# Token lists of six experts in a mixture-of-experts stage: the marks as moving operand through four column strips

## What is computed

```python
capacity = max(1, int(Sz * CAP_FACTOR / E) + 1)          # 313 of 1250
scores = jax.nn.softmax(jnp.einsum('bsd,ed->bse', x, router_w), axis=-1)
gate_vals, sel_idx = jax.lax.top_k(jnp.swapaxes(scores, 1, 2), capacity)
tokens = x[b_idx, sel_idx]
h = jax.nn.gelu(jnp.einsum('becd,edh->bech', tokens, w1) + b1[None, :, None, :], approximate=False)
y = jnp.einsum('bech,ehd->becd', h, w2) + b2[None, :, None, :]
out = jnp.zeros_like(x).at[b_idx, sel_idx].add(y * gate_vals[..., None])
```

## Time and profile before

| | us |
|---|---|
| median of 3 runs (lowest, highest) | 1502.46 (1500.67, 1502.67) |
| the profiled execution | 1499.6 |
| its span, first to last instruction | 1497.5 |
| TensorE busy | 1422.4 (95%) |
| VectorE busy | 883.5 (59%) |
| ScalarE, GpSimd busy | 544.7, 357.6 |
| mean granted TensorE clock | 0.986 of 2.4 GHz |
| expert stage, from the first layer of expert 0 to the end | 1255.4 to 1497.5 |
| one expert of the first six | 29.19 |

### The profile page before, as it was taken

How to read it: one execution, slowest core, us unless ns; L and a number is a source line. 1 busy time by engine, 2 the same in 40 slices (tenths; PEclk the granted TensorE clock), 3 DMA queues, 4 the chain that set the end, 5 groups by cost and what they waited for, 6 DMA issues and landing times.

```text
span 1497.5 us, 28303 instructions
## 1 busy us (share of the span) xinstructions
PE 1422.4 (95%) x8379; PEld 726.7 (49%) x8379; DVE 883.5 (59%) x1992; ACT 544.7 (36%) x756; POOL 357.6 (24%) x372
## 2 busy tenths in 40 slices
PE   6789999999999999999999999999999979999996
PEld 5334444545444444444654444446544435666653
DVE  7888888686987887541442222223336676576652
ACT  4578757373524543210111210001111124565651
POOL 4332320202201110000874002800012311343232
PEclk9999999999999999999999999999999999999998
DMA  7242010000275555553323443430046756789963
GB/s 282 43 86 51 8 43 14 28 0 28 72 205 155 159 168 174 144 142 112 128 72 90 103 101 125 170 114 12 0 128 177 203 190 200 218 250 273 282 163 56
DMA packets 156674, 185.95 MB, mean 124 GB/s; under 512 B 106172, under 2 KB 107659, under 8 KB 156600
## 3 DMA queue, kind: packets, MB, share of 16 engines
q1 hardware_dynamic: 144440, 143.07, 31.4%
q0 software_dynamic: 12160, 41.95, 10.8%
HBM read 118.40 MB, written 41.94 MB: 107 GB/s over the span
## 4 chain that ended last, share of the span: by engine, by line
PE 67%; DVE 12%; issue 8%; DMA 4%; ACT 3%; SPq 2%; DVEq 2%; POOL 1%; ACTq 0%; POOLq 0%
PE ps L1340 26%; PE ps L1408 11%; PE ps L1547 7%; PE ps L1567 6%; PE ps L1240 3%; PE ps L1242 3%; PE ps L1241 3%; DMA cr<-self_d 2%; SPq L907 1%; PE ps L1573 1%; PE ps L1171 1%; PE ps L1535 1%; ACT th L1651 1%; DVE hm L2018 1%; DVE wa L1979 1%
## 5 line engine op out<-in xcount | busy, mean ns | idle before, releaser
L1340 PE MATMUL ps<-wa,tb 128*128 128x512 f16 x960 | 210.3, 381 | 4.4 <-issue 4.4
L1408 PE MATMUL ps<-adj,nm 128*128 128x384 f16 (+2 forms) x960 | 169.6, 340 | 1.6 <-DVEq L2333 1.6
L1240 PE MATMUL ps<-gp,hop 128*128 (+1 forms) x400 | 151.6, 379 | 1.0 <-DVE gn L2092 1.0
L1242 PE MATMUL ps<-gp,hop 128*128 (+1 forms) x400 | 151.6, 379 | 0.0
L1241 PE MATMUL ps<-gp,hop 128*128 (+1 forms) x400 | 151.6, 379 | 0.0
L1340 PEld LDWEIGHTS ps<-wa,tb 128*128 (+1 forms) x960 | 93.7, 98 | 117.8 <-issue 7.6
L1408 PEld LDWEIGHTS ps<-adj,nm 128*128 x960 | 93.9, 98 | 77.2 <-issue 2.1
L1761 ACT ACTIVATE tb<-cx 128x384 f32 (+1 forms) x48 | 26.8, 559 | 276.8 <-DVE cx L2323 276.8
L1340 PE MATMUL ps<-wa,hop 128*128 128x512 f16 x480 | 106.9, 383 | 2.9 <-DVEq L2267 2.9
L1340 PE MATMUL ps<-wb,tb 128*128 128x512 f16 x480 | 103.8, 379 | 1.6 <-DVEq L2347 1.6
L1340 PE MATMUL ps<-wb,hop 128*128 128x512 f16 x480 | 105.3, 383 | 0.0
(11 more groups left out here) (392 smaller groups left out, 2218.9 us busy)
## 6 DMA issues: line engine op xcount, KB each, us to landing
w_st<-in_ew SPq DMA_DIRECT2D x16, 2048.0 KB, 11.0
self_d<-cr SPq DMA_DIRECT2D x20, 512.0 KB, 2.9
cr<-self_d SPq DMA_DIRECT2D x20, 512.0 KB, 3.8
stage<-in_wn POOLq DMA_DIRECT2D x16, 512.0 KB, 3.8
x_d<-cr SPq DMA_DIRECT2D x10, 512.0 KB, 4.7
cx<-x_d SPq DMA_DIRECT2D x10, 512.0 KB, 4.1
cr<-x_d SPq DMA_DIRECT2D x10, 512.0 KB, 4.0
out<-cr SPq DMA_DIRECT2D x10, 512.0 KB, 3.0
```

What stands on the lines that cost most here:

```text
L1240: pe.matmul(acc, wh, gh, start=(s_ == 0), stop=False, skip_group_check=True)
L1242: return pe.matmul(acc, wl, gh, start=False, stop=(s_ == NT - 1), skip_group_check=True)
L1340: ins = pe.matmul(ps[:, b + c, :], lhs(part, k), w[:, w_, k, c * 512:(c + 1) * 512], start=(k == 0 and part == 0 and w_ == 0), stop=(last ...
L1408: ins = pe.matmul(ps[:, 6 + j, 0:n], nm[:, part, s_, bass.ds(f * P, P)], adj[:, s_, t0 * TP:t0 * TP + n], start=first, stop=(s_ == NT - 1 ...
```

## The change

For the six experts 2 to 7 the two operands change places. The marks of a tile (384 columns) are the moving operand, and the stationary one is `tokg[:, t]`, 128 tokens by 32 columns: four numbers of all eight experts. The ten tiles go through four 32-column strips of the array in turn (tile t to strip t % 4), so `ps[32q:32q+32, 0, 0:384]` holds partial lists. ScalarE copies these 128x384 numbers to `strip_lists` (`strips_out`, between the gating of chunks 0 and 1). Three products, a function `slots`, then take `strip_lists` as stationary operand and four columns of `strip_sum`, a constant that adds the four strips and picks expert e, into `ps[:, 0, 384:396]`. `slots` stands behind the 64-row tail of `ffn2`, so VectorE's `lists` is moved behind all three evacuations, and `places` behind it. The constant is made by two more GpSimd operations in the setup. Diff, cut to its core:

```diff
+            link(g.tensor_tensor(strip_sum[:], ident16[:, 0:64].rearrange("p (a n) -> p a n", a=2),
+                                 ident16[:, 64:128].rearrange("p (a n) -> p a n", a=2), ALU.add))
+            link(g.tensor_tensor(strip_sum[:, 0], strip_sum[:, 0], strip_sum[:, 1], ALU.add))
...
                 pe.wait_ge(s_sel, e - 1)
                 pe.wait_ge(s_eev, 6 * e + 2)
+                pe.sem_inc(s_tick, 1)
+                for t in range(NT):
+                    q = t % 4
+                    ins = pe.matmul(ps[32 * q:32 * q + 32, 0, 0:3 * P], tokg[:, t].rearrange("p e n -> p (e n)"), selm[:, t, :],
+                                    start=(t < 4), stop=(t >= NT - 4), skip_group_check=True, tile_position=(0, 32 * q))
+                    if t >= NT - 4:
+                        ins.then_inc(s_strips, 1)
+
+            def slots(i, j):
+                e = 2 * i + j
+                pe.wait_ge(s_stripped, e)
+                pe.sem_inc(s_tick, 1)
+                of = strip_sum[:, 0].rearrange("p (e n) -> p e n", n=4)
                 for c in range(3):
-                    for t in range(NT):
-                        ins = pe.matmul(ps[:, 0, 4 * c:4 * c + 4], selm[:, t, c * P:(c + 1) * P],
-                                        tokg[:, t, e, :] if isinstance(e, int) else tile_of(tokg[:, t], e),
-                                        start=(t == 0), stop=(t == NT - 1))
+                    ins = pe.matmul(ps[:, 0, 384 + 4 * c:388 + 4 * c], strip_lists[:, c * P:(c + 1) * P],
+                                    of[:, e, :] if isinstance(e, int) else tile_of(of, e),
+                                    start=(c == 0), stop=(c == 2), skip_group_check=True)
                 ins.then_inc(s_lst, 1)
...
                 ffn2(i, j, (lambda: lists(i + 1, j)) if more else none)
+                if more:
+                    slots(i + 1, j)
...
+            def strips_out(i, j):
+                s.wait_ge(s_strips, 4 * (2 * i + j) - 3)
+                s.sem_inc(s_tick, 1)
+                s.activation(strip_lists, ps[:, 0, 0:3 * P], ACT.Copy).then_inc(s_stripped, 1)
...
                 for c in range(3):
+                    if c == 1:
+                        between()
...
-                out(i, j, 0)
+                out(i, j, 0), out(i, j, 1), out(i, j, 2)
                 if more:
                     lists(i + 1, j)
-                out(i, j, 1)
                 if more == 2:
                     places(*after(i + 1, j))
-                out(i, j, 2), low(*n, 1)
+                low(*n, 1)
```

More of the change, by code:

```diff
@@ L261, in build @@
         sel = sb("sel", [P, 4, 8], F32)
+        strip_sum = sb("strip_sum", [P, 2, 4 * NE], F16)
         stage = sb("stage", [P, 2, 1024], F32)
@@ L470, in build @@
         eb2t = spare[:, NT * 3 * P + 4 * D:NT * 3 * P + 6 * D].bitcast(F32).rearrange("p (j n) -> p j n", j=2)
+        strips_at = NT * 3 * P + 6 * D
+        strip_lists = spare[:, strips_at:strips_at + 3 * P]
         gE.close()
@@ L542, in build @@
         s_tick, s_wsh = sem("s_tick"), sem("s_wsh")
+        s_strips, s_stripped = s_candT, s_row
         def rows(ap, t, n=1):
@@ L1836, in hidden, with gates @@
                     s.activation(hT[:, 0, h, 0:FW], hb[:, h, 0:FW], ACT.Copy, scale=SA).then_inc(s_ehi, 1)
-            def gates(i, j):
+            def strips_out(i, j):
+                s.wait_ge(s_strips, 4 * (2 * i + j) - 3)
+                s.sem_inc(s_tick, 1)
+                s.activation(strip_lists, ps[:, 0, 0:3 * P], ACT.Copy).then_inc(s_stripped, 1)
+            def gates(i, j, between=none):
                 e = 2 * i + j
                 for c in range(3):
+                    if c == 1:
+                        between()
                     s.wait_ge(s_y, 5 * e + min(2 * c + 2, 5) + 2)
@@ L1846, in body @@
                 n = after(i, j)
-                high(*n, 0), hidden(i, j), turn(*n), high(*n, 1), gates(i, j)
+                high(*n, 0), hidden(i, j), turn(*n), high(*n, 1)
+                gates(i, j, (lambda: strips_out(i + 1, j)) if more else none)
             s.wait_ge(s_sc, NT)
@@ L2500, in lists @@
                 v.wait_ge(s_lst, e + 1)
-                link(v.tensor_copy(lst[:, j].rearrange("p c n -> p (c n)"), ps[:, 0, 0:12]))
+                at = 0 if isinstance(e, int) and e < 2 else 384
+                link(v.tensor_copy(lst[:, j].rearrange("p c n -> p (c n)"), ps[:, 0, at:at + 12]))
                 v.tensor_tensor(idx[:, j, :], lst[:, j, :, 0], pads[:], ALU.add).then_inc(s_idx, 1)
```

## The result

| | before | after |
|---|---|---|
| median of 6 runs (lowest, highest), us | 1500.56 (1499.09, 1502.67) | 1555.45 (1552.40, 1561.62) |
| ratio, 95% interval | | 1.0373 (1.0356 to 1.0390) |
| profiled execution, us | 1499.6 | 1561.6 |
| TensorE busy, us | 1422.4 | 1436.0 |
| GpSimd busy, us | 357.6 | 395.3 |

The changed kernel is 54.9 us slower (1555.45-1500.56); forecast were 45 us. The page of after: TensorE's share falls from 95% to 92%, and a group that stood among the small ones is now one of the costliest, the gathers, 3212 ns each. (Line, engine, operation, count | busy us, mean ns | idle before.)

The account below looks back on a forecast made before the run. TensorE was taken to bound the expert stage alone, 29.19 us an expert. A 5.4 us wait plus 2.1 us of clock gave 7.5 us, six times, 45 us: 1544.6 by the profiled run, 1547 by the median; 8-in-10 range 1508 to 1558.

Parts of the forecast that it names:

- the likeliest case: Gather and scatters held by VectorE's remainders, and TensorE's clock falls: 1538 to 1556 us, forecast 1547, chance 54%.
- signs of being wrong: Third gather takes 1 us, scatters land before T+18, or TensorE's gap stands elsewhere, at the transposes for instance.
- The wait forecast at the second half: Second layer's second half starts at T+26.7 in place of T+21.28, 5.4 us late, behind VectorE's evacuation awaiting scatter landing.
- TensorE's part: Per expert: thirty small products removed, 0.73 us; strips add 0.48, slots 0.07; saves 0.18, 1.1 for six.
- The times of the list: After the tail: list copy T+0.77, row numbers T+1.14, list done T+1.62; gathers start T+2.03, T+3.32, T+4.61.
- T: The moment at which the previous expert's last product, its 64-row tail, ends on TensorE and the next first layer starts.
- The short case behind expert 5: No marks, remainders start at T+1.65, first two gathers held instead of the third; third scatter out at T+18.3 all the same.
- By the scatter above it ends ... after the remainder does: T+9.35: Third gather, started inside the remainder of T+4.2 to T+8.6, is held until just behind that remainder's end.
- What it delays is swallowed by the later wait: Third gather lands some 5 us after T+9.35, about when its transposes want it (T+14.5); no added cost.
- Landing: Third scatter, done at T+18.3, lands 7.6 us after its end, T+25.9, and then VectorE's first evacuation can begin.
- The upper row: Scatter of 1404.00 in the profile before: landed 12.2 us after its start, 8.0 after its end, with weights in flight.
- The clock: TensorE's clock falls at T+24.1, rises at T+30.9; work from T+26.7 runs 4.2 us at half speed, losing 2.1.

Follow-up runs that it names:

- The VectorE order alone: Kernel before with only VectorE's list and marks moved behind its third evacuation, ahead of the weight remainders, thirty list products kept: 1558.06 us against 1500.28, ratio 1.0381.
- all else alone: Changed kernel with strips early, slots where the thirty products stood and VectorE's order of before: 1495.49 us against 1500.28, ratio 0.9964; again 1494.12, ratio 0.9963.
- the unused constant: Kernel before plus only the two GpSimd operations that make the constant, which nothing uses: 1496.82 us against 1501.04, ratio 0.9972.
- the run with the pause: Changed kernel with one tiny VectorE memset, and a wait for its end, between the two weight remainders: 1556.37 us, ratio 1.0362.

## Why the prediction was right, and where it was not

- **The time** lies in the range of 8 in 10, 1508 to 1558, and just in the likeliest case, 1538 to 1556. This is luck in part: by one of the prediction's own signs of being wrong, "if TensorE's gap stands elsewhere, at the transposes for instance", the path was wrong, since that is where the gap stands. Two other signs failed too: the third gather does not end just behind a remainder's end, and the first scatter is not held (1.65 us). The wait forecast at the second half, 5.4 us each time, was 3.1 us in all, and a wait that was put at nothing stood at the transposes, 7.9 to 10.1 us behind each of experts 0 to 4.
- **The bound and the cause** were right: TensorE alone before, and the loss made by GpSimd's DMAs, started late, meeting VectorE's remainders. The VectorE order alone gives 1.0381, all else alone no more than the unused constant does.
- **TensorE's part**: forecast strips 0.48 and slots 0.07, measured 0.59 and 0.05 to 0.09. The saving of 0.18 us an expert was too high; with the early order it is nil (29.22 for 29.19).
- **The times of the list** came out to within 0.3 us: row numbers at T+1.0, third gather at T+4.5 (forecast T+4.61). (The T-7.5 that the prediction has for the list before is that of the row numbers; the gates were done at T-7.0.) The short case behind expert 5 was right as well: third scatter out at T+18.0, forecast T+18.3.
- **"By the scatter above it ends ... after the remainder does: T+9.35"**: this step failed. One held scatter was taken as the rule. The third gather ended at T+14.7 after a hold through both remainders, between which nothing paused; with a pause it took 4.68 us. The pause is not the only thing that decides, as the gathers released without one show.
- **"What it delays is swallowed by the later wait"**: this fell with it. The gather landed 8.2 us after its end, not 5, and TensorE waited 8.35 us at the transposes, before the wait that I had priced. Of the waits in after 47.1 us are the gathers' and 3.1 the evacuation's.
- **Landing**: forecast 7.6 us after the third scatter's end at T+18.3, T+25.9. It ended at T+20.4 and released the evacuation at T+31.4, 11 us behind. The upper row had 8.0; that three scatters and two loads of weights now flew together was in the argument but hardly in the number.
- **The clock** was forecast at 2.1 us an expert. It cost 13.1 us over the stage, 2.2 for each of six. It did not become dearer with the longer wait, since the low stretch is partly waited away: in the body of expert 1 it lasted from 1302.0 to 1312.3, and TensorE stood idle for the first 3.9 of these 10.2 us.
- **The sum**: 45 forecast, 54.9 measured by the medians, 62.0 by the profiled executions. The forecast waits were 32 us, the measured 50. In the run with the pause, where the gather is released about as forecast, the time is still 1556, the scatters land 11.2 us after their start, not 9.2, and the gathers cost 12.1 us of waits, not none: on the forecast's own path, landing was the term that was sized too small.

## What to carry to other kernels

A step that TensorE does not wait for can still be a place in a queue that matters: before moving it, write down which DMAs its result starts, and which long VectorE instructions and which transfers they will then meet. Cutting a VectorE instruction in pieces let GpSimd in behind one expert of six here, a short pause did behind all; but when two waits stand side by side, taking one away shows the other at nearly the same price. And a gain of 0.3% is to be set against a control that has the change's side products only.

## What the runs showed of the hardware that was not expected

- A GpSimd indirect DMA was not always let in between two adjacent VectorE instructions. Gathers that started 0.51 to 0.77 us into the first remainder were held through both and the hidden parts (9.94 to 10.27 us, five times in after); ones that started 0.31 to 0.38 us or about 1.2 us into one were released at its end (4.94 and 3.96 us). With eight pieces of 1.1 us five were held throughout and three were let in between pieces. With a tiny instruction and a wait for its end between the remainders, which left them 0.06 to 0.19 us apart, all five were released. What decides is open.
- A one-input VectorE operation from 32-bit to 16-bit, 4096 columns in 2.28 us, held a gather that had started 0.8 us before it: 3.22 us, and 5.44 us where a second such operation followed at once.
- In the changed kernel, scatters that add to HBM landed 10.7 to 13.7 us after their start where two loads of 2 MB were issued ahead of them, 6.7 to 8.2 where it was one, and the third scatter 8.0 with a quarter of each; a load of 2 MB took 18.2 us in the median of after, 11.0 before.
- TensorE's ten products in four 32-column strips took 59 ns each where eighty in three strips took 42. What the change of tiling costs of it was not measured apart.
